# Keys of two sequence tiles multiplied at once, turned as they are made, from blocks of the key matrix that stay in TensorE

## The chip, the cores and the metric

One core of a Trainium2 chip runs the whole program. The metric is device time in microseconds (us) of one execution, the median of several. TensorE (PE) multiplies and turns (transposes) matrices, ScalarE (ACT) and VectorE (DVE) do elementwise work and move results out of TensorE's accumulators, GpSimd (POOL) does small arithmetic, and SyncE (SP) issues the DMAs. Each engine runs its own instructions in order and waits for the others at semaphores.

## The reference, cut to what matters

`x` and `ctx` have 32 tiles of 128 rows and 1024 columns. Each tile passes through four layers:

```
x = x + attention0(layernorm(x), ctx)     # 64-wide queries and keys from ctx, softmax over 1024
x = x + ffn(layernorm(x), routed scales, sign(weight))
x = x + attention1(layernorm(x), ctx)     # Q = text Wq^T + bq, K = ctx Wk^T + bk, 1024 wide
x = x + lora(layernorm(x), routed)
```

The change concerns attention1. Its scores are `(text Wq^T + bq)(ctx Wk^T + bk)^T / 32`. The kernel folds the two weight matrices into one, M = Wk^T Wq, so that per tile it needs "keys through queries", `kw = ctx M` (128 by 1024), and from these the scores `text (kw + bias)^T`.

## The kernel before

The program has a setup, which among other things computes M in two parts, a rounded one (`m_hi`) and a remainder (`m_low`), and then a software pipeline over the 32 tiles. Iteration k prepares tile b = k (queries, keys and values of attention0), attends for tile a = k - 1 (softmax and values of attention0), and runs the chain of the other three layers for tile c = k - 2. Three iterations are unrolled ahead of a hardware loop over the rest, and two after it drain the pipeline. What each engine does in which order is written by hand in its `body`; there is no scheduler.

Products that need precision are split into rounded float32 parts ("hi" and "lo", type F32R), three products for one.

**The keys.** `keys_through_queries` goes through 16 units per tile (two halves of the 1024 columns, eight blocks of 128 rows of M each). A unit is three products of 512 columns: the stationary operand is a turned block of the context (`cT_hi` or `cT_lo`, 128 by 128), the columns that stream are `m_hi`, which lies on chip, or `m_ring`, eight slots into which SP streams the remainder from memory. The units are spread over the first part of an iteration, between the `query_scores` of tile a (`KW_UNITS`). ACT moves the two finished halves to `kw`. In the steps s = 0 to 7 that follow, each with `key_scores`, an exponential on ACT (`prob`), its rounding (`p_hi`), the remainder on DVE (`p_lo`), a running sum (`p_sum`) and `weigh_values` on PE, the kernel turns `kw` on PE, four blocks at s = 4 and four at s = 6, and DVE adds the bias while it moves them to `kwT` (`keys_turned`). At s = 4 the scores of attention1 for tile c read `kwT` of the iteration before.

**The end of an iteration.** At s = 6 ACT takes the softmax of attention1 (`attn`), PE turns it, ACT moves it to `attnT`; between the two ACT normalizes the next tile (`normalize(0)`). At s = 7 PE multiplies `attnT` with the context, makes the queries and keys of tile b (`wqkT`), sums the exponentials with `ones`, turns the context of tile b (`c_in`, eight blocks), and turns the sums (`denominator_columns`) that DVE has moved to `den_wide`. Then come the last `weigh_values`, the turned denominators, the turned `xn_3`, `values` and the first keys' units of tile b. DVE, ahead of `den_wide`, adds the attention to `res` and takes its statistics.

Of the kernel before, what the change touches and what calls it, by code (L numbers as in the profile page):

```python
# [18 lines left out]
F32 = mybir.dt.float32  # L19
# [29 lines left out]
def build(nc, x, ctx_, wq0, bq0, wk0, bk0, wv0, bv0, w_ffn, b_ffn, gate, ics, ocs,  # L49
# [13 lines left out]
    with top:  # L63
# [35 lines left out]
        m_hi = sb("m_hi", [P, T, D], F32R)  # L99
        with ExitStack() as before:  # L100
            wk_nat_late = sb("wk_nat_late", [P, T, HALF], F32, before)
        with ExitStack() as before:
            wk_lo_late = sb("wk_lo_late", [P, T, HALF], F32R, before)
        SLOTS = 8
        m_ring = sb("m_ring", [P, SLOTS, HALF], F32R)
        m_low = nc.dram_tensor("m_low", [2 * T, P, HALF], F32, kind="Internal").ap()
# [16 lines left out]
        with ExitStack() as tmp:  # L123
# [65 lines left out]
            with nc.Block() as block:  # L189
                @block.sync  # L190
                def _(sp):
# [25 lines left out]
                    for n, (kind, i) in enumerate(groups):  # L217
                        if kind == "m":
                            sp.wait_ge(copied, evicted_by_dve(n + 1))
                            sp.dma_start(m_low[(i % 2) * T + f_order[i // 2]],  # L220
                                         m_stage[:, i % STAGES, :].bitcast(F32)).then_inc(m_stored[i % STAGES], 16)
# [9 lines left out]
                    for s in range(STAGES):  # L231
                        sp.wait_ge(m_stored[s], 16 * 2 * T // STAGES)
# [42 lines left out]
                def _(dve):  # L275
# [45 lines left out]
                    for n, (kind, i) in enumerate(groups):  # L321
# [24 lines left out]
                        elif kind == "m":  # L346
                            dve.wait_ge(m_hi_made, i + 1)
                            if i >= STAGES:
                                dve.wait_ge(m_stored[i % STAGES], 16 * (i // STAGES))
# [117 lines left out]
        cT_hi = sb("cT_hi", [P, T, P], F32R)  # L467
        cT_lo = sb("cT_lo", [P, T, P], F32R)

# [6 lines left out]
        kw = x1  # L476
        kwT = sb("kwT", [P, T, P])
# [70 lines left out]
        kwT_done = sem("kwT_done")  # L548
# [33 lines left out]
        kwT_ready = sem("kwT_ready")  # L582
# [37 lines left out]

        def tile4(buf, h):

            return buf[:, 4 * h:4 * h + 4, :].rearrange("p t c -> p (t c)")
# [10 lines left out]
        def iterations(engine, body):  # L634
            for k in range(3):
                body(k, True, k >= 1, k >= 2)
            with engine.Fori(3, NB) as k:
                body(k, True, True, True)
            body(NB, False, True, True)
            body(NB + 1, False, False, True)  # L640

        with nc.Block() as block:
# [3 lines left out]
            def _(sp):  # L646
                def low_unit(u):
                    sp.dma_start(m_ring[:, u % SLOTS, :].bitcast(F32), m_low[u]).then_inc(m_loaded[u % SLOTS], 16)

                def body(k, prepare, attend, chain):  # L650
# [4 lines left out]
                    if attend:  # L655
                        for u in range(12, 16):
                            sp.wait_ge(kw_unit_done, nth(16, a, u - SLOTS + 1))
                            low_unit(u)
                    if prepare:
                        for u in range(SLOTS):  # L660
                            if attend:
                                sp.wait_ge(kw_unit_done, nth(16, a, u + SLOTS + 1))
                            low_unit(u)
                    if prepare and attend:
                        sp.wait_ge(ffn_done, nth(2, c, 2))
                        sp.wait_ge(cT_done, nth(2, b - 1, 2))
                        sp.dma_start(c_in[:, :], ctx_[b]).then_inc(c_loaded, 16)
                        sp.wait_ge(v_done, nth(2, b - 1, 2))
                        sp.dma_start(xn[:, :], x[b]).then_inc(xn_loaded, 16)
                    if attend:  # L670
                        sp.wait_ge(kwT_done, nth(2, a, 2))
                        sp.dma_start(x1[:, :], x[a]).then_inc(x1_loaded, 16)
# [5 lines left out]
                    if prepare:  # L678
                        for u in range(8, 12):
                            sp.wait_ge(kw_unit_done, nth(16, b, u - SLOTS + 1))  # L680
                            low_unit(u)
# [9 lines left out]
            def _(pool):  # L691
# [16 lines left out]
                def body(k, prepare, attend, chain):  # L708
# [20 lines left out]
            def _(act):  # L729
# [27 lines left out]
                def body(k, prepare, attend, chain):  # L757
# [16 lines left out]
                    if attend:  # L774
                        act.wait_ge(kw_unit_done, nth(16, a, 8))
                        act.wait_ge(biased, nth(1, a - 1, 1))
                        nc.scalar.activation(kw[:, half(0)], acc[:, half(0)], ACT.Identity).then_inc(kw_ready, 1)
# [10 lines left out]
                    if attend:  # L788
                        act.wait_ge(kw_unit_done, nth(16, a, 16))
                        nc.scalar.activation(kw[:, half(1)], acc[:, half(1)], ACT.Identity).then_inc(kw_ready, 1)  # L790
                    for s in range(T):
# [41 lines left out]
                    if prepare:  # L833
                        act.wait_ge(cT_done, nth(2, b, 1))
                        act.wait_ge(kw_unit_done, nth(16, b - 1, 16))
                        nc.scalar.activation(tile4(cT_hi, 0), shared[0][:, :], ACT.Identity).then_inc(cT_hi_ready, 1)
                        act.wait_ge(cT_done, nth(2, b, 2))
                        nc.scalar.activation(tile4(cT_hi, 1), shared[1][:, :], ACT.Identity).then_inc(cT_hi_ready, 1)
# [40 lines left out]
            def _(dve):  # L879
# [72 lines left out]
                def keys_turned(a, h):  # L952

                    dve.wait_ge(sc1_done, nth(1, a - 1, 1))
                    dve.wait_ge(kwT_done, nth(2, a, 2 - h))
                    nc.vector.tensor_tensor(kwT[:, 4 * h:4 * h + 4, :], shared[h][:, :].rearrange("p (t c) -> p t c", t=4),
# [516 lines left out]
```

## Time and profile before

| | us |
|---|---|
| median of 3 runs (2147.27 to 2150.97) | 2148.87 |
| the profiled execution's own time | 2148.65 |
| its span, first to last instruction | 2146.7 |
| TensorE busy (matmuls), of the span | 2120.8 |
| VectorE busy | 1852.8 |
| ScalarE busy | 1161.2 |

A matmul's record is longer than the distance to the next one: matmuls are pipelined and their ends are modelled. What a matmul costs in a stream is the distance from start to start. For a group of n records that is (length of the group - length of one) / (n - 1). Weight loads have an engine of their own in the profile (PEld), since they run beside the matmuls.

### The profile page before, as it was taken

To read this page: it belongs to the slowest core of one execution; us is meant where nothing else is said; L and a number is where in the kernel's file an instruction comes from. 1 tells how busy PE (TensorE), PEld (TensorE's weight loads), DVE (VectorE), ACT (ScalarE), POOL (GpSimd) and SP (SyncE) were. 2 spreads that over 40 slices of the span, in tenths; PEclk is the share of its full clock that TensorE was granted. 3 is DMA by queue.
4 is the path that set the end of the run, shared out by engine and by line. 5 is a ranking of instruction groups with operands and counts; after the bars stand their busy time and mean duration, and the time that the engine had idled before them with its cause. 6 is when DMAs were issued, how large, how long until landed. Compare 5 with 4: busy or idle time off the path is not lost.

```text
span 2146.7 us, 35672 instructions
## 1 busy us (share of the span) xinstructions
PE 2120.8 (99%) x11479; PEld 1665.8 (78%) x11479; DVE 1852.8 (86%) x3097; ACT 1161.2 (54%) x1722; POOL 263.8 (12%) x306
## 2 busy tenths in 40 slices
PE   9989999999999999999999999999999999999998
PEld 7867777777777777787777778777777777777776
DVE  8268898988888998888898988889898888899884
ACT  4145555655555565555555655555566555555542
POOL 0011111111101110111111111111111110111010
PEclk9999999999999999999999999999999999999999
DMA  6344343233443323334332333434323344332320
GB/s 215 146 157 128 118 135 103 93 119 127 127 135 119 112 93 107 127 127 137 117 127 100 95 127 117 137 121 133 107 88 117 127 127 137 117 119 93 100 69 30
DMA packets 110874, 254.03 MB, mean 118 GB/s; under 512 B 12976, under 2 KB 14272, under 8 KB 110848
## 3 DMA queue, kind: packets, MB, share of 16 engines
q1 hardware_dynamic: 110848, 253.69, 36.5%
q8 instruction: 16, 0.26, 0.1%
q14 instruction: 10, 0.08, 0.0%
HBM read 215.89 MB, written 20.97 MB: 110 GB/s over the span
## 4 chain that ended last, share of the span: by engine, by line
PE 91%; DVE 1%; ACT 1%; issue 1%; DMA 0%; POOL 0%; DVEq 0%; POOLq 0%; ACTq 0%
PE acc L1239 17%; PE shared L1168 7%; PE scores L1188 6%; PE acc L1199 6%; PE shared L1213 6%; PE acc L1202 6%; PE acc L1200 6%; PE shared L1214 6%; PE scores L1228 5%; PE scores L1227 5%; PE shared L1428 3%; PE shared L1354 3%; PE scores L1174 3%; PE scores L1377 3%; PE scores L1384 1%; PE scores L1404 1%
## 5 line engine op out<-in xcount | busy, mean ns | idle before, releaser
L1033 DVE TENSOR_TENSOR p_lo<-prob,p_hi 128x1024 fp32r<-128x1024 f32 x256 | 312.5, 1221 | 103.7 <-ACT p_hi L805 85.9
L798 ACT ACTIVATE prob<-scores 128x1024 f32<-128x1024 f32 x256 | 260.6, 1018 | 236.6 <-PE scores L1228 185.4
L901 DVE TENSOR_REDUCE neg_max<-scores 128x1 f32<-128x1024 f32 x256 | 307.0, 1221 | 42.1 <-PE scores L1188 35.6
L704 POOL TENSOR_TENSOR rstd<-var_eps,minus_half 128x1 f32<-128x1 f32 x128 | 126.9, 992 | 1732.0 <-DVE var_eps L891 1732.0
L805 ACT ACTIVATE p_hi<-prob 128x1024 fp32r<-128x1024 f32 x256 | 271.2, 1059 | 42.8 <-PE acc L1239 38.6
L1199 PE MATMUL acc<-m_hi,cT_hi 128*128 128x512 f32 x512 | 217.5, 425 | 0.9 <-DVE x L935 0.9
L1213 PE MATMUL shared<-signT,y_hi 128*128 128x512 f32 x512 | 204.5, 399 | 2.2 <-ACT oscale L787 2.2
L1227 PE MATMUL scores<-q_hl,k_hh 128*128 128x512 f32 x512 | 201.4, 393 | 1.9 <-DVE q_m L1015 1.5
L1202 PE MATMUL acc<-m_ring,cT_hi 128*128 128x512 f32 x512 | 202.9, 396 | 0.0
L1200 PE MATMUL acc<-m_hi,cT_lo 128*128 128x512 f32 x512 | 202.4, 395 | 0.0
L1228 PE MATMUL scores<-q_m,k_l 128*128 128x512 f32 x512 | 202.2, 395 | 0.0
L1214 PE MATMUL shared<-signT,y_lo 128*128 128x512 f32 x512 | 201.7, 394 | 0.0
L1041 DVE TENSOR_TENSOR p_sum<-p_sum,prob 128x1024 f32<-128x1024 f32 x160 | 195.1, 1220 | 0.0
L1239 PE MATMUL acc<-p_hi,v_hi 128*128 128x512 f32 x512 | 171.0, 415 | 4.4 <-DVE p_lo L1033 3.9
L1188 PE MATMUL scores<-k_hh,q_hl 128*128 128x512 f32 x512 | 165.4, 404 | 0.3 <-issue 0.3
L1239 PE MATMUL acc<-p_hi,v_lo 128*128 128x512 f32 x512 | 161.0, 396 | 0.0
L1239 PE MATMUL acc<-p_lo,v_hi 128*128 128x512 f32 x512 | 160.9, 395 | 0.0
L1227 PEld LDWEIGHTS scores<-q_hl,k_hh 128*128 128x128 f32 x512 | 96.1, 188 | 25.6 <-issue 1.6
L1188 PEld LDWEIGHTS scores<-k_hh,q_hl 128*128 128x128 f32 x512 | 91.5, 188 | 30.9 <-issue 6.8
L1213 PEld LDWEIGHTS shared<-signT,y_hi 128*128 128x128 f32 x512 | 96.3, 188 | 23.6 <-issue 2.4
L1239 PEld LDWEIGHTS acc<-p_lo,v_hi 128*128 128x128 f32 x512 | 96.0, 188 | 23.5
L1202 PEld LDWEIGHTS acc<-m_ring,cT_hi 128*128 128x128 f32 x512 | 96.2, 188 | 23.2
(241 smaller groups left out, 4211.6 us busy)
## 6 DMA issues: line engine op xcount, KB each, us to landing
m_ring<-m_low SPq DMA_DIRECT2D x512, 256.0 KB, 3.1
c_in<-in_ctx SPq DMA_DIRECT2D x32, 512.0 KB, 3.3
xn<-in_x SPq DMA_DIRECT2D x32, 512.0 KB, 4.1
x<-in_x SPq DMA_DIRECT2D x32, 512.0 KB, 3.2
c_val<-in_ctx SPq DMA_DIRECT2D x32, 512.0 KB, 3.6
out_x<-oscale SPq DMA_DIRECT2D x32, 512.0 KB, 3.0
q_m<-q_hl SPq DMA_DIRECT2D x32, 256.0 KB, 3.1
k_hh<-k_hh SPq DMA_DIRECT2D x32, 256.0 KB, 3.5
```

The costliest lines, as they stand in the source:

```text
L805: nc.scalar.activation(p_hi[s % 2][:, :], prob[s % 2][:, :], ACT.Identity).then_inc(p_hi_ready, 1)
L901: nc.vector.tensor_reduce(neg_max[:, t:t + 1], scores[t % 2][:, :], AX_X, ALU.max, negate=True).then_inc(row_max, 1)
L1033: nc.vector.tensor_tensor(p_lo[s % 2][:, :], prob[s % 2][:, :], p_hi[s % 2][:, :].bitcast(F32), ALU.subtract).then_inc(p_lo_ready, 1)
L1188: last = mm(scores[t % 2][:, half(h)], q_hl[:, t * P:(t + 1) * P], k_hh[:, half(h)], start=True, stop=True)
L1199: mm(acc[:, half(h)], cT_hi[:, f, :], m_hi[:, f, half(h)], start=f == 0, stop=False)
L1200: mm(acc[:, half(h)], cT_lo[:, f, :], m_hi[:, f, half(h)], start=False, stop=False)
L1202: mm(acc[:, half(h)], cT_hi[:, f, :], m_ring[:, u % SLOTS, :], start=False, stop=f == T - 1).then_inc(kw_unit_done, 1)
L1213: mm(shared[h][:, :], y_hi[:, f, :], signT[:, f, half(h)], start=f == 0, stop=False)
L1214: last = mm(shared[h][:, :], y_lo[:, f, :], signT[:, f, half(h)], start=False, stop=f == T - 1)
L1227: mm(scores[s % 2][:, half(h)], k_hh[:, s * P:(s + 1) * P], q_hl[:, half(h)], start=True, stop=False)
L1228: last = mm(scores[s % 2][:, half(h)], k_l1[:, s * P:(s + 1) * P], q_m[:, half(h)], start=False, stop=True)
L1239: last = mm(acc[:, half(h)], v[:, s, :], p[s % 2][:, half(h)], start=first, stop=end)
```

## The change

Tiles are taken in pairs (an even and an odd one), and the keys of both are made together and already turned. The stationary operand of a product is now a 128 by 128 block of M, rounded part or remainder, and what streams is the turned context of the two tiles side by side, 256 columns. Each iteration makes four of the eight feature blocks, for both tiles. A unit has two blocks of rows of M, in both parts, six products; there are 16 units per iteration, as before, and 256 KB per unit, as before. M's rounded part is no longer kept on chip; both parts come through `m_ring`. ACT adds the bias when it moves the finished keys: in an iteration that attends an even tile to `kw_first`, from where an SP DMA copies them to `kwT`, and in the next to `kwT` directly. The turning of `kw` on PE and `keys_turned` on DVE are gone.

Both contexts of a pair must be turned and split before the first of its keys. An iteration with an even tile b therefore turns two contexts: the odd tile's (`c_odd`) at s = 4 and s = 6, and `c_in` at s = 7 as before. An iteration with an odd tile turns none. The hardware loop has two iterations in its body.

```diff
-        SLOTS = 8
-        m_ring = sb("m_ring", [P, SLOTS, HALF], F32R)
+        SLOTS = 8
+        m_ring = sb("m_ring", [P, SLOTS, 2, 2, P], F32R)
+        cT_hi = sb("cT_hi", [P, T, 2, P], F32R)
+        cT_lo = sb("cT_lo", [P, T, 2, P], F32R)
+        kwT = sb("kwT", [P, T, 2, P])
+        kw_first = sb("kw_first", [P, TS, 2, P])
+        c_odd = sb("c_odd", [P, D])
```

SP's queue in an iteration, where `odd` is the parity of tile b:

```diff
+                    if prepare and not odd:
+                        sp.wait_ge(qk_done, nth(2, b - 1, 2))
+                        sp.dma_start(c_odd[:, :], ctx_[b + 1]).then_inc(c_odd_loaded, 16)
...
+                    if attend and odd:
+                        sp.wait_ge(kw_ready, nth(2, a, 2))
+                        sp.wait_ge(sc1_done, nth(1, c, 1))
+                        sp.dma_start(kwT[:, 0:TS, :, :].rearrange("p f j s -> p (f j s)"),
+                                     kw_first[:, :, :, :].rearrange("p f j s -> p (f j s)")).then_inc(kw_moved, 16)
```

ACT's two new functions, and its step s:

```diff
+                def turned_keys(a, odd, h):
+                    act.wait_ge(kw_unit_done, nth(16, a, 8 * h + 8))
...
+                    for f in range(2 * h, 2 * h + 2):
+                        to = kwT[:, TS + f, :, :] if odd else kw_first[:, f, :, :]
+                        last = nc.scalar.activation(to.rearrange("p j s -> p (j s)"), acc[:, f * 2 * P:(f + 1) * 2 * P], ACT.Identity,
+                                                    bias=key_bias[:, TS * odd + f:TS * odd + f + 1])
+                    last.then_inc(kw_ready, 1)
+                def context_rounded(k, j, h, n):
+                    act.wait_ge(cT_done, turned_contexts(k, n))
+                    act.wait_ge(kw_unit_done, nth(16, k - 1, 16))
+                    nc.scalar.activation(of_pair(cT_hi, j, h), bank4(shared[h]), ACT.Identity).then_inc(cT_hi_ready, 1)
...
+                        if chain and prepare and not odd and s == 6:
+                            context_rounded(k, 1, 1, 1)
                         if attend:
                             act.wait_ge(exp_ready, nth(8, a, s + 1))
...
-                        if prepare and attend and s == 6:
+                        if prepare and attend and s == 6 and (odd or not chain):
                             normalize(0, b, xn, xn)
                         if chain and s == 6:
                             act.wait_ge(attnT_done, nth(1, c, 1))
...
+                        if chain and prepare and not odd and s == 6:
+                            context_rounded(k, 1, 0, 2)
+                            normalize(0, b, xn, xn)
```

DVE's step s:

```diff
-                        if attend and s in (4, 6):
-                            keys_turned(a, (6 - s) // 2)
+                        if chain and prepare and not odd and s in (5, 6):
+                            context_remainder(k, 1, 6 - s, s - 4)
```

PE, a unit of the keys, and steps 4, 6 and 7 (`ahead` is `chain and prepare and not odd`):

```diff
-                        mm(acc[:, half(h)], cT_hi[:, f, :], m_hi[:, f, half(h)], start=f == 0, stop=False)
-                        mm(acc[:, half(h)], cT_lo[:, f, :], m_hi[:, f, half(h)], start=False, stop=False)
                         pe.wait_ge(m_loaded[u % SLOTS], nth(32, a, 16 * (u // SLOTS + 1)))
-                        mm(acc[:, half(h)], cT_hi[:, f, :], m_ring[:, u % SLOTS, :], start=False,
-                           stop=f == T - 1).then_inc(kw_unit_done, 1)
+                        to = acc[:, f * 2 * P:(f + 1) * 2 * P]
+                        for j in range(2):
+                            g = 2 * (u % TS) + j
+                            hi, lo = m_ring[:, u % SLOTS, 0, j, :], m_ring[:, u % SLOTS, 1, j, :]
+                            rows_hi, rows_lo = (rows[:, g, :, :].rearrange("p j s -> p (j s)") for rows in (cT_hi, cT_lo))
+                            mm(to, hi, rows_hi, start=g == 0, stop=False)
+                            mm(to, hi, rows_lo, start=False, stop=False)
+                            last = mm(to, lo, rows_hi, start=False, stop=g == T - 1)
+                        last.then_inc(kw_unit_done, 1)
...
-                        if attend and s == 4:
-                            transposes(1, kw, kwT_done)
+                        if ahead and s == 4:
+                            pe.wait_ge(c_odd_loaded, nth(8, b, 16))
+                            transposes(1, c_odd, cT_done)
...
-                        if attend and s == 6:
-                            transposes(0, kw, kwT_done)
+                        if ahead and s == 6:
+                            transposes(0, c_odd, cT_done)
...
-                        if prepare and s == 7:
+                        if prepare and not odd and s == 7:
                             pe.wait_ge(x3_ready, nth(2, c, 2))
```

How it moves instructions, first on PE at s = 4 of the loop's iteration: `kwT` and `key_col` make the scores of attention1, `x` is the buffer in which `kw` lies, and `p_hi`, `p_lo` belong to `weigh_values`. Before:

```order
L1354 MATMUL shared<-kwT,xnT 128x128 x8
L1355 MATMUL shared<-ident,key_col 128x128
L1168 MATMUL shared<-ident,x 128x128 x4
L1239 MATMUL acc<-p_hi,v_hi 128x512 x2
L1239 MATMUL acc<-p_hi,v_lo 128x512 x2
L1239 MATMUL acc<-p_lo,v_hi 128x512 x2
```

and now, in an iteration with an odd tile b:

```order
L1419 MATMUL shared<-kwT,xnT 128x128 x8
L1420 MATMUL shared<-ident,key_col 128x128
L1302 MATMUL acc<-p_hi,v_hi 128x512 x2
L1302 MATMUL acc<-p_hi,v_lo 128x512 x2
L1302 MATMUL acc<-p_lo,v_hi 128x512 x2
```

The four turns between the scores and `weigh_values` are gone there; in an iteration with an even b four turns of `c_odd` stand in their place. It is the same at s = 6. Next, PE at s = 7, from the sums of exponentials (`ones`) to the last `weigh_values`; `xnT` is the buffer of `den_wide`. Before:

```order
L1380 ISA
L1384 MATMUL scores<-p_sum,ones 32x256 x4
L1384 MATMUL scores<-prob,ones 32x256 x4
L1168 MATMUL shared<-ident,c_in 128x128 x8
L1245 MATMUL scores<-ident,xnT 128x128 x2
L1239 MATMUL acc<-p_hi,v_hi 128x512 x2
```

and now, with an odd b:

```order
L1452 ISA
L1456 MATMUL scores<-p_sum,ones 32x256 x4
L1456 MATMUL scores<-prob,ones 32x256 x4
L1308 MATMUL scores<-ident,xnT 128x128 x2
L1302 MATMUL acc<-p_hi,v_hi 128x512 x2
```

The eight turns of `c_in` between the sums and the turned sums are gone; with an even b they stand as before. Third, ACT from the rounding of step 6 to the exponential of step 7 (`prob`). Before:

```order
L805 ACTIVATE p_hi<-prob 128x1024
L813 ACTIVATE r_bias<-r_max 128x1
L816 ACTIVATE attn,r_sum<-shared,r_bias 128x128
L731 REGISTER_ALU
L732 ACTIVATE xn<-xn,shift,rstd 128x1024
L823 ACTIVATE attnT<-shared 128x128
L795 REGISTER_ALU
L797 REGISTER_ALU
L798 ACTIVATE prob<-scores 128x1024
```

and now, in an iteration with an even b:

```order
L811 ACTIVATE cT_hi<-shared 128x4x128
L860 ACTIVATE p_hi<-prob 128x1024
L868 ACTIVATE r_bias<-r_max 128x1
L871 ACTIVATE attn,r_sum<-shared,r_bias 128x128
L878 ACTIVATE attnT<-shared 128x128
L809 REGISTER_ALU
L811 ACTIVATE cT_hi<-shared 128x4x128
L767 REGISTER_ALU
L768 ACTIVATE xn<-xn,shift,rstd 128x1024
L848 REGISTER_ALU
L850 REGISTER_ALU
L851 ACTIVATE prob<-scores 128x1024
```

Two roundings of the odd context (`cT_hi`) came in, and the normalizing of `xn` went from ahead of `attnT` to behind it. With an odd b ACT has the order of before.

## Rows read from the trace of the kernel before

**Rows 1.** The page: span, and each engine's busy time.

```profile
span 2146.7 us, 35672 instructions
...
PE 2120.8 (99%) x11479; PEld 1665.8 (78%) x11479; DVE 1852.8 (86%) x3097; ACT 1161.2 (54%) x1722; POOL 263.8 (12%) x306
```

**Rows 2.** Timeline, steady state, the keys' products: start us, length us, engine, line, operation.

```profile
1001.22 0.40 PE L1199 MATMUL acc<-m_hi,cT_hi 128*128 128x512 f32 x1
1001.22 0.19 PEld L1200 LDWEIGHTS acc<-m_hi,cT_lo 128*128 128x128 f32 x1
1001.46 0.39 PE L1200 MATMUL acc<-m_hi,cT_lo 128*128 128x512 f32 x1
...
1001.91 0.39 PE L1199 MATMUL acc<-m_hi,cT_hi 128*128 128x512 f32 x1
```

**Rows 3.** Groups by line and shape, TensorE: count, busy us in total, mean ns of one.

```profile
L1354 PE MATMUL shared<-kwT,xnT 128*128 128x128 f32 x512 | 62.4, 275 | 0.0
L1377 PE MATMUL scores<-c_in,wqkT 128*128 128x512 f32 x128 | 60.2, 593 | 1.5 <-PEq L189 1.5
...
L1295 PE MATMUL shared<-route3T,ics 96*128 96x128 f32 x256 | 32.3, 269 | 0.0
```

**Rows 4.** The same view for TensorE's weight loads, one line.

```profile
L1354 PEld LDWEIGHTS shared<-kwT,xnT 128*128 128x128 f32 x512 | 62.0, 192 | 2.7
```

**Rows 5.** Page, DMA issues: KB each, us to landing.

```profile
m_ring<-m_low SPq DMA_DIRECT2D x512, 256.0 KB, 3.1
```

**Rows 6.** Timeline of one period, score steps 4 to 7, TensorE, ScalarE and VectorE.

```profile
1025.37 0.60 PE L1168 MATMUL shared<-ident,x 128*128 128x128 f32 x4
...
1025.73 0.71 PE L1239 MATMUL acc<-p_hi,v_hi 128*128 128x512 f32 x2
...
1025.93 1.03 ACT L798 ACTIVATE prob<-scores 128x1024 f32<-128x1024 f32 x1 [1.52 <-DVE p_sum L1041]
...
1027.46 1.06 ACT L805 ACTIVATE p_hi<-prob 128x1024 fp32r<-128x1024 f32 x1 [0.50 <-PE acc L1239]
...
1028.64 0.37 ACT L816 ACTIVATE attn<-shared,r_bias 128x128 f32<-128x128 f32 x1
...
1029.00 1.23 ACT L732 ACTIVATE xn<-xn,shift,rstd 128x1024 f32<-128x1024 f32 x1
...
1029.53 0.27 PE L1364 MATMUL shared<-ident,attn 128*128 128x128 f32 x1
...
1029.64 0.60 PE L1168 MATMUL shared<-ident,x 128*128 128x128 f32 x4
...
1030.14 0.26 ACT L823 ACTIVATE attnT<-shared 128x128 f32<-128x128 f32 x1
...
1030.29 1.03 ACT L798 ACTIVATE prob<-scores 128x1024 f32<-128x1024 f32 x1
...
1032.50 1.23 DVE L1033 TENSOR_TENSOR p_lo<-prob,p_hi 128x1024 fp32r<-128x1024 f32 x1 [0.59 <-DVE r_inv L1070]
```

**Rows 7.** Timeline, the end of that period.

```profile
1033.64 1.40 DVE L1075 SCALAR_TENSOR_TENSOR res<-shared,r_inv,res 128x512 f32<-128x512 f32 x2
...
1036.24 1.09 PE L1168 MATMUL shared<-ident,c_in 128*128 128x128 f32 x8
...
1036.79 0.42 DVE L922 COPY xnT<-scores 128x256 f32<-128x256 f32 x1
...
1037.26 0.44 PE L1245 MATMUL scores<-ident,xnT 128*128 128x128 f32 x2
1037.32 0.60 ACT L836 ACTIVATE cT_hi<-shared 128x512 fp32r<-128x512 f32 x1
...
1039.81 1.22 PE L1168 MATMUL shared<-ident,p_sum 128*128 128x128 f32 x8
```

**Rows 8.** Timeline of the first iteration.

```profile
122.48 3.09 PE L1174 MATMUL scores<-wvT,xn 128*128 128x128 f32 x16 [2.44 <-ACT xn L732]
...
123.08 1.29 DVE L1099 TENSOR_TENSOR cT_lo<-shared,cT_hi 128x512 fp32r<-128x512 f32 x2 [1.85 <-ACT cT_hi L836]
```

More of the change, by code:

```diff
@@ L634, in iterations @@
         def iterations(engine, body):
[L635 to L640, printed above, removed]
+            for k in range(4):
+                body(k, k % 2, True, k >= 1, k >= 2)
+            with engine.Fori(4, NB - 1, 2) as k:
+                body(k, 0, True, True, True)
+                body(k + 1, 1, True, True, True)
+            body(NB, 0, False, True, True)
+            body(NB + 1, 1, False, False, True)
         with nc.Block() as block:
@@ L774, in body @@
                     if attend:
-                        act.wait_ge(kw_unit_done, nth(16, a, 8))
-                        act.wait_ge(biased, nth(1, a - 1, 1))
-                        nc.scalar.activation(kw[:, half(0)], acc[:, half(0)], ACT.Identity).then_inc(kw_ready, 1)
+                        turned_keys(a, 1 - odd, 0)
                     if chain:
@@ L788, in body @@
                     if attend:
-                        act.wait_ge(kw_unit_done, nth(16, a, 16))
-                        nc.scalar.activation(kw[:, half(1)], acc[:, half(1)], ACT.Identity).then_inc(kw_ready, 1)
+                        turned_keys(a, 1 - odd, 1)
                     for s in range(T):
@@ L832, in body @@
                         normalize(0, b, xn, xn)
[L833 to L838, printed above, removed]
+                    if prepare and not attend:
+                        context_rounded(k, 1, 1, 1)
+                        context_rounded(k, 1, 0, 2)
+                    if prepare and not odd:
+                        context_rounded(k, 0, 0, 3)
+                        context_rounded(k, 0, 1, 4)
                     if attend and not prepare:
@@ L1095, in body @@
                         denominators_inverse(a)
-                    if prepare:
-                        for h in range(2):
-                            dve.wait_ge(cT_hi_ready, nth(2, b, h + 1))
-                            nc.vector.tensor_tensor(tile4(cT_lo, h), shared[h][:, :], tile4(cT_hi, h).bitcast(F32),
-                                                    ALU.subtract).then_inc(cT_lo_ready, 1)
+                    if prepare and not attend:
+                        context_remainder(k, 1, 1, 1)
+                        context_remainder(k, 1, 0, 2)
+                    if prepare and not odd:
+                        context_remainder(k, 0, 0, 3)
+                        context_remainder(k, 0, 1, 4)
                     if attend:
@@ L1257, in out_products, with body @@
                     mm(banks[1], lowT_lo[:, :], bT_hi[:, half(1)], start=False, stop=True).then_inc(out_done, 1)
-                def body(k, prepare, attend, chain):
+                def body(k, odd, prepare, attend, chain):
                     b, a, c = k, k - 1, k - 2
+                    ahead = chain and prepare and not odd
                     last_chain = chain and not attend
```

130 lines of the change are left out of this document (79 added, 51 removed).

## The prediction

> **What bounds the kernel now.** I read the page first. TensorE is busy for 2120.8 of 2146.7 us, VectorE for 1852.8, ScalarE for 1161.2 [rows 1]. The reader is to see that nothing can be gained that does not shorten TensorE's own chain, and that VectorE has so little to spare that places may exist where TensorE just manages not to wait for it. So I read two things next: what one matmul costs in a stream, and, in the timeline of one steady iteration, who releases whom where the change adds or removes work. The profiled execution took 2148.65 us, 0.2 below the median of 2148.87; all sums below start from 2148.65. A difference under 0.2% (4.3 us) is what a measurement here can hardly tell from none.
>
> **The keys' products.** Before, a unit is three products of 512 columns, and the next unit starts 0.69 us after this one's start (1001.22 to 1001.91), so a product costs 0.23 us [rows 2]. An iteration has 16 units, 11.04 us. Now it has 96 products of 256 columns: the same columns, twice as many weight loads. The question is what a product of half the length costs, and the trace has no such row. The neighbours, with the distances worked out from the groups: the scores with `kwT` are unsplit float32, 16 records in each of 32 groups, 62.4 / 32 = 1.95 us, so (1.95 - 0.275) / 15 = 0.112 us per pass of 128 columns, each pass with a load of 128 by 128. The context with `wqkT` (4 records in 1.88 us) gives 0.429 us per pass of 512. The routed scales (`ics`, F32R by the code, 8 in 1.01 us) give 0.106 us for 128 columns [rows 3]. So a load can be had every 0.112 us and less, although one load's record is 192 ns long: 512 of them fill only 62.0 us [rows 4], they overlap each other and the matmuls. The passes of unsplit float32 grow by (0.429 - 0.112) / 384 = 0.000826 us per column; an F32R product streams in about half of that, 0.211 us for 512 columns, which leaves 0.019 us of the 0.23 that could be a fixed price per product.
>
> The ends: 0.106 us, if a half-length product goes as fast as the loads do (96 x 0.106 = 10.18 us, 0.86 less per iteration, 28 us less over 32); 0.125 us, if the 0.019 us is fixed (12.0 us, 0.96 more, 31 us more over 32). I take 0.115, half of the long product: the unsplit passes change weights as often, and the line through their two lengths leaves only 0.112 - 128 x 0.000826 = 0.006 us fixed, so the rest seems to go with the F32R columns. By this the term is **0**.
>
> The load of the next product's weights starts at the same time as the product itself (both 1001.22), and the next product follows 0.24 us later, less than load and product one after the other [rows 2]. The Trainium skill ("TensorE: Matmul & The Clock Gate", Part 3, The mechanism) says that a weight load overlaps a running matmul only when the two are in different row groups; here all use the whole array, so each load would stand alone, and 48 more of them per iteration would be paid in full. This trace does not agree with that. The Trainium skill gives in the same page (LDWEIGHTS) columns / 1.2 ns for a load, 107 ns for 128 columns; an estimate from it is that load and product of 256 columns would be about equally long, and the sum by it that of the lower end.
>
> **The ring.** Both parts of M now come through it, in units as large and as many as before; one lands 3.1 us after its issue [rows 5], and eight slots are 5.5 us of keys at least. Only the first two products of a unit lose their freedom to start ahead of the landing. 0 taken. The copy from `kw_first` and the load of `c_odd` are needed half an iteration or more after their issue: 0.
>
> **Iterations with an odd b.** No turns stand at s = 4, 6 and 7. The four at s = 4 held `weigh_values` up from 1025.37 to 1025.73, 0.36 us. ACT's rounding of step 6 waits for that `weigh_values` (1027.46, idle 0.50 for PE's `acc`), so it comes 0.36 earlier, and after it all that ACT does in one chain: `attn` 1028.64, `normalize` 1029.00, `attnT` 1030.14, the exponential of step 7 at 1030.29; then DVE's `p_lo` at 1032.50, which had idled 0.59 [rows 6]. From there DVE goes on without a gap: `res` 1033.64, statistics, `den_wide` 1036.79 to 1037.21, and PE's turned sums start at 1037.26 [rows 7]. So the turned sums wait for DVE's chain, not for the eight turns of `c_in` ahead of them (1036.24, 1.09 us), which only fill that wait. Removing those, and the four at s = 6, moves PE's wait and not its end: of about 1.8 us of turns, 0.36 us counts. Behind it, the turns of `xn_3` no longer wait for the remainder of a context (1.22 us for eight where `c_in` has 1.09): 0.13 more. Sum **-0.49 us** for each of 15 such iterations, -7.4 us. VectorE's `keys_turned` and two remainders are gone too, but the chain above hangs on ACT there, so this is hidden.
>
> **Iterations with an even b.** PE has the same turns at the same places. ACT gets two roundings of 0.60 us (the length of `cT_hi` in [rows 7]) and another order, and the chain above runs over ACT. The first rounding follows the exponential of step 6 (1025.93, done 1026.96) and fills most of ACT's idle 0.50: the rounding `p_hi` goes from 1027.46 to 1027.6. `attn` is done at 1029.15. Now `attnT` is next, and PE turns `attn` at 1029.53 to 1029.80, because `weigh_values` stands ahead of it: ACT idles until 1029.9, a gap that `normalize` used to fill. Then the second rounding has to wait for the turns of `c_odd` (1029.64 to 1030.24), runs 1030.34 to 1030.94, and `normalize` comes only then, at 1030.91. Before, what followed `normalize` on ACT (`attnT` then) started 1.14 us after it (1029.00 to 1030.14); now the exponential of step 7 follows. So it starts at 1032.05 in place of 1030.29: 1.76 us late [rows 6]. Late next are `p_lo` of step 7 (DVE waits on it in order), `res`, the statistics, `den_wide` (1038.55), the turned sums (1039.02), and with them the last `weigh_values`, the turned denominators, `xn_3` and `values`, which PE runs without a wait from there [rows 7]. `c_in` waits for `res` until 1036.9 and is done by 1038, inside that wait. Sum **+1.76 us** for each of 15 such iterations (k = 2 to 30), +26.4 us.
>
> **The ends of the pipeline.** In the first iteration both contexts are turned, rounded and split one after the other, through the same two accumulators: `values` stood at 122.48, the remainders of the one context at 123.08 to 124.37 [rows 8]; the second context's turns (1.04 us, by the distance of `c_in` to the next in [rows 7]: 1.02) come behind these, so `values` starts at about 125.5: **+3.0 us**. Iterations 1 and 32 lose key turns: -0.5 each as above, -1.0. The setup stores M's rounded part too, in shorter rows; its products take all the time there: 0, at most some 3 us (a landing of [rows 5]).
>
> **Sum.** 26.4 - 7.4 + 3.0 - 1.0 + 0 = +21.0 us: 2148.65 + 21.0 = 2169.7, **2170 us**.
>
> **Rivals.**
> *The half-length product goes at 0.106 us.* For it: the `ics` row, which is F32R and has that distance. Against it: those products have 96 rows and 128 columns, so they show loads and not a stream of 256. Then 2170 - 28 = 2142 us, faster; the time falls 0.2% below the old one from 0.107 us down.
> *Loads don't hide behind half-length products.* Product and load one after the other would be 0.115 + 0.112 = 0.227 us, 96 of them 21.8 us, 10.75 us more per iteration, 344 us: 2514 us. Against it: 0.112 us for load and pass together [rows 3]. (By the rule of the Trainium skill on row groups, "TensorE: Matmul & The Clock Gate", Part 3, it would come out this way.)
> *The even iterations' slip is swallowed*, because PE has other work to wait for or ACT gets ahead: then only the odd ones change, 2148.65 - 7.4 + 2.0 = 2143 us. Against it: DVE's `den_wide` ends 0.05 us ahead of the turned sums; there is no slack that could swallow it.
>
> **How the numbers follow.** Forecast 0.66, with 2155 to 2201 us by the ends of the half-length product that still end slower; rival one 0.08, loads not hidden 0.07, slip swallowed 0.07; 0.08 for a mixture that ends within 0.2% of before, 0.04 for slower ones between. So faster 0.15, same 0.08, slower 0.77. The range is 2142 to 2205: it reaches down to the first two faster cases and up to the higher price of the product with the setup's 3 us; below it lie some 0.09, above it, with the unhidden loads, 0.10.
>
> **What the profile after would show.** The distance between products of 256 columns at the keys' line: 0.115 us or another. Iterations alternating, the even longer by about 2.2 us than the odd. In the even ones, ACT's `normalize` after the second `cT_hi`, PE idle about 1 us ahead of the turned sums, and the exponential of step 7 some 1.8 us later behind the turning of `attn`. In the odd ones PE idle ahead of the turned sums too, for `den_wide`. The prediction is wrong if the half-length product costs other than 0.106 to 0.125 us, or if PE's wait at the turned sums does not follow ACT's step 7.

## The result, and the profile after

The changed kernel takes 2166.73 us (median of 4 runs, 2165.79 to 2166.94), the kernel before in the same session 2148.07 (4 runs, 2146.58 to 2150.97): ratio 1.0084, 95% interval 1.0067 to 1.0102. It is slower by 0.8%, where 2170 us was forecast.

The page of the changed kernel: span, busy time of each engine, and the shares of the chain that ended last.

```profile
span 2163.9 us, 37822 instructions
...
PE 2093.0 (97%) x12759; PEld 1728.1 (80%) x12759; DVE 1812.5 (84%) x3033; ACT 1179.5 (55%) x1786; POOL 264.3 (12%) x306
...
PE 75%; DVE 11%; issue 6%; ACT 3%; ACTq 0%; DVEq 0%; POOL 0%; POOLq 0%
```

Against [rows 1], TensorE has 28 us less work and the span is 17.2 us longer: TensorE now waits. To see where, I use one instruction as a mark, the turn of the row maxima, which each iteration has once. Its rows in the timeline of before, and then of after (start, length, engine, line):

```profile
940.72 0.27 PE L1314 MATMUL scores<-ident,neg_max 128*8 128x128 f32 x1
...
1002.79 0.27 PE L1314 MATMUL scores<-ident,neg_max 128*8 128x128 f32 x1
...
1064.85 0.27 PE L1314 MATMUL scores<-ident,neg_max 128*8 128x128 f32 x1
```

```profile
950.22 0.27 PE L1378 MATMUL scores<-ident,neg_max 128*8 128x128 f32 x1
...
1013.92 0.27 PE L1378 MATMUL scores<-ident,neg_max 128*8 128x128 f32 x1
...
1075.44 0.27 PE L1378 MATMUL scores<-ident,neg_max 128*8 128x128 f32 x1
```

Before, every iteration takes 62.07 us. After, one with an even tile b takes 63.70 (950.22 to 1013.92) and one with an odd tile 61.52, and so through the whole steady part (means 63.71 and 61.53): +1.64 and -0.54. All of the steady loss lies in the even ones.

Steps 6 and 7 of that even iteration, timeline of after; the times to compare are distances from the mark (here 950.22, in [rows 6, 7] 1002.79):

```profile
974.90 1.06 ACT L860 ACTIVATE p_hi<-prob 128x1024 fp32r<-128x1024 f32 x1
...
976.08 0.37 ACT L871 ACTIVATE attn<-shared,r_bias 128x128 f32<-128x128 f32 x1
...
977.26 0.28 ACT L878 ACTIVATE attnT<-shared 128x128 f32<-128x128 f32 x1 [0.71 <-PE shared L1431]
...
977.69 0.60 ACT L811 ACTIVATE cT_hi<-shared 128x512 fp32r<-128x512 f32 x1 [0.16 <-PE shared L1224]
...
978.19 1.23 ACT L768 ACTIVATE xn<-xn,shift,rstd 128x1024 f32<-128x1024 f32 x1
...
979.32 1.01 ACT L851 ACTIVATE prob<-scores 128x1024 f32<-128x1024 f32 x1
...
981.51 1.23 DVE L1088 TENSOR_TENSOR p_lo<-prob,p_hi 128x1024 fp32r<-128x1024 f32 x1 [2.18 <-issue]
...
985.79 0.42 DVE L980 COPY xnT<-scores 128x256 f32<-128x256 f32 x1
...
986.27 0.44 PE L1308 MATMUL scores<-ident,xnT 128*128 128x128 f32 x2 [1.06 <-DVE xnT L980]
...
988.82 1.22 PE L1224 MATMUL shared<-ident,p_sum 128*128 128x128 f32 x8
```

`p_hi` of step 6 and `attn` stand where they stood (24.68 and 25.86 us after the mark; before 24.67 and 25.85). Then ScalarE idles 0.71 for the turn of `attn`, rounds the context, and only then normalizes. The exponential of step 7 starts 29.10 after the mark, before 27.50: 1.60 late. `p_lo` is 1.58 late, the wide denominators (the copy to `xnT`, L980) 1.57, the turned sums at L1308 1.58, the turns of `xn_3` (they lie in the buffer `p_sum`, L1224) 1.58. The loss is handed on whole from ScalarE over VectorE to TensorE.

The end of the odd iteration that follows, same view (mark 1013.92):

```profile
1047.48 0.42 DVE L980 COPY xnT<-scores 128x256 f32<-128x256 f32 x1
...
1047.96 0.44 PE L1308 MATMUL scores<-ident,xnT 128*128 128x128 f32 x2 [1.11 <-DVE xnT L980]
...
1050.51 1.04 PE L1224 MATMUL shared<-ident,p_sum 128*128 128x128 f32 x8
```

The turned sums start 34.04 after the mark, before 34.47, and TensorE waits 1.11 for them although no turn is left ahead of them. The waits of TensorE in the whole of after (waiting line, releaser, us in total, times, longest) say the same of both kinds:

```profile
PE scores L1308 <- DVE xnT L980: 33.1, 31, 1.1
```

Before had no such wait of TensorE in its list. No landing of `m_ring` or `kwT` stands in the list of after either, so the ring and the copy cost TensorE no wait that the profile shows. The keys' products of after, grouped by line, and a few in the timeline:

```profile
L1263 PE MATMUL acc<-cT_hi,m_ring 128*128 128x256 f32 x1024 | 302.6, 296 | 0.9 <-DVE x L993 0.9
L1264 PE MATMUL acc<-cT_lo,m_ring 128*128 128x256 f32 x1024 | 288.6, 282 | 0.0
...
L1264 PEld LDWEIGHTS acc<-cT_lo,m_ring 128*128 128x128 f32 x1024 | 194.5, 190 | 7.4
```

```profile
1012.71 0.28 PE L1263 MATMUL acc<-cT_hi,m_ring 128*128 128x256 f32 x1
1012.83 0.28 PE L1264 MATMUL acc<-cT_lo,m_ring 128*128 128x256 f32 x1
1012.95 0.28 PE L1265 MATMUL acc<-cT_hi,m_ring 128*128 128x256 f32 x1
```

One product of 256 columns follows the other after 0.12 us, with a load whose record is 0.19 us long. The loads are hidden: 3072 products that each stood behind their load would show in these distances.

### The profile page after: what moved, and what is told of

Same layout as the page of the kernel before. It is cut to its first block, busy times and chain, and to the rows that moved or that the text cites. A ratio compares the mean times of both kernels' runs of the same rounds, so it can differ in the third digit from the quotient of the medians.

```text
span 2163.9 us, 37822 instructions
## 1 busy us (share of the span) xinstructions
PE 2093.0 (97%) x12759; PEld 1728.1 (80%) x12759; DVE 1812.5 (84%) x3033; ACT 1179.5 (55%) x1786; POOL 264.3 (12%) x306
## 4 chain that ended last, share of the span: by engine, by line
PE 75%; DVE 11%; issue 6%; ACT 3%; ACTq 0%; DVEq 0%; POOL 0%; POOLq 0%
PE acc L1302 11%; PE scores L1244 6%; PE acc L1263 6%; PE shared L1276 6%; PE acc L1264 6%; PE acc L1265 6%; PE shared L1277 5%; PE shared L1224 5%; PE scores L1291 5%; PE scores L1290 5%; DVE p_lo L1088 3%; PE shared L1506 3%; PE scores L1230 3%; DVE res L1130 2%; DVE stat L945 1%
## 5 line engine op out<-in xcount | busy, mean ns | idle before, releaser
L1263 PE MATMUL acc<-cT_hi,m_ring 128*128 128x256 f32 x1024 | 302.6, 296 | 0.9 <-DVE x L993 0.9
L1264 PE MATMUL acc<-cT_lo,m_ring 128*128 128x256 f32 x1024 | 288.6, 282 | 0.0
L1265 PE MATMUL acc<-cT_hi,m_ring 128*128 128x256 f32 x1024 | 288.5, 282 | 0.0
L1263 PEld LDWEIGHTS acc<-cT_hi,m_ring 128*128 128x128 f32 x1024 | 195.7, 191 | 8.5 <-DVE x L993 1.1
L1264 PEld LDWEIGHTS acc<-cT_lo,m_ring 128*128 128x128 f32 x1024 | 194.5, 190 | 7.4
L1265 PEld LDWEIGHTS acc<-cT_hi,m_ring 128*128 128x128 f32 x1024 | 194.2, 190 | 0.0
```

The lines of the kernel that those rows point to most:

```text
L1263: mm(to, hi, rows_hi, start=g == 0, stop=False)
L1264: mm(to, hi, rows_lo, start=False, stop=False)
L1265: last = mm(to, lo, rows_hi, start=False, stop=g == T - 1)
```

## The experiments

The theory was the prediction's: ScalarE's order at step 6 of the even iterations (normalize behind `attnT` and a rounding) makes the exponential of step 7 late, and that is what the even iterations lose; the odd ones gain the four turns of step 4, the other turns being idle time of TensorE anyway. The rivals: ScalarE's order is covered by other waits, and the loss is the turning of a second context on TensorE or VectorE, or the half-length products.

All times below are medians; the ratio is to the kernel before in the same session.

**Normalize ahead again.** Edit to the changed kernel:

```diff
-                        if prepare and attend and s == 6 and (odd or not chain):
+                        if prepare and attend and s == 6:
                             normalize(0, b, xn, xn)
...
                             context_rounded(k, 1, 0, 2)
-                            normalize(0, b, xn, xn)
```

> In iterations with an even b ACT normalizes the next tile ahead of attnT again, as in the kernel before; the second rounding of the odd context stays behind attnT. Theory (the even iterations are longer because ACT idles between attn and attnT and then does the second rounding and normalize ahead of the exponential of step 7): that exponential comes at about 1031.0 instead of some 1.6 us after its old place of 1030.29, so 0.7 us late instead of 1.6; 0.9 us off each of 15 even iterations, 13.5 us: about 2153 us. Rival (the time went to the half-length products or to the ring, and ACT's order is beside the way): no change, 2165 to 2168 us.

Measured 2150.53 us, ratio 1.0012 (1.0002 to 1.0022): 16.2 us less than the changed kernel. Timeline of this kernel, even iteration, mark at 945.09:

```profile
971.31 1.23 ACT L768 ACTIVATE xn<-xn,shift,rstd 128x1024 f32<-128x1024 f32 x1
...
972.44 0.27 ACT L878 ACTIVATE attnT<-shared 128x128 f32<-128x128 f32 x1
...
972.60 0.60 ACT L811 ACTIVATE cT_hi<-shared 128x512 fp32r<-128x512 f32 x1
...
973.08 1.03 ACT L851 ACTIVATE prob<-scores 128x1024 f32<-128x1024 f32 x1
...
980.04 0.44 PE L1307 MATMUL scores<-ident,xnT 128*128 128x128 f32 x2 [0.41 <-DVE xnT L979]
```

Normalize runs in the gap in which TensorE turns `attn`, and ScalarE does not idle. The exponential starts 27.99 after the mark, 0.49 later than before, and the turned sums 0.48 later. What is left fits the one rounding that still stands ahead of it (972.60 to 973.08, 0.48 from start to start). The even iteration takes 62.60, 1.11 less than in the changed kernel; the odd one 61.52, unchanged.

**Normalize last.** Normalize goes behind the rounding of step 7's probabilities, in every iteration, and the second rounding behind the exponential of step 7:

```diff
-                        if chain and prepare and not odd and s == 6:
-                            context_rounded(k, 1, 1, 1)
+                        if chain and prepare and not odd and s >= 6:
+                            context_rounded(k, 1, 7 - s, s - 5)
...
+                        if prepare and attend and s == 7:
+                            normalize(0, b, xn, xn)
...
-                        if prepare and attend and s == 6 and (odd or not chain):
-                            normalize(0, b, xn, xn)
...
-                        if chain and prepare and not odd and s == 6:
-                            context_rounded(k, 1, 0, 2)
-                            normalize(0, b, xn, xn)
```

> ACT normalizes the next tile behind the rounding of step 7 in all iterations, where it waits for the queries otherwise, and the second rounding of the odd context stands between the exponential and the rounding of step 7. Nothing is left out. Theory: attnT follows attn as soon as PE has turned it, the exponential of step 7 comes about 0.3 us ahead of its old place, and the second rounding costs 0.6 behind it. Even iterations then end some 0.35 us behind those of the kernel before instead of 1.64, odd ones 0.3 us earlier than now, -0.86 instead of -0.55: 1.6 us for each of 15 pairs, 24 us: about 2143 us. Rival (ACT's order is beside the way): 2165 to 2168 us. A middle result, 2150 to 2158, if VectorE and not ACT holds step 7 once ACT is early.

Measured 2140.39 us, ratio 0.9968 (0.9956 to 0.9979). It is the only version of the changed kernel with all its work that pays: 26.3 us below the changed kernel and 7.5 below the kernel before in its session (2147.87). Timeline of this kernel, even iteration, mark at 940.13:

```profile
967.18 0.28 ACT L878 ACTIVATE attnT<-shared 128x128 f32<-128x128 f32 x1 [0.73 <-PE shared L1428]
...
967.39 1.03 ACT L851 ACTIVATE prob<-scores 128x1024 f32<-128x1024 f32 x1
...
968.32 0.59 ACT L811 ACTIVATE cT_hi<-shared 128x512 fp32r<-128x512 f32 x1
...
968.79 1.06 ACT L860 ACTIVATE p_hi<-prob 128x1024 fp32r<-128x1024 f32 x1
...
969.74 1.24 ACT L768 ACTIVATE xn<-xn,shift,rstd 128x1024 f32<-128x1024 f32 x1
969.90 1.02 PE L1437 MATMUL shared<-c_val,attnT 128*128 128x512 f32 x2
969.94 1.23 DVE L1085 TENSOR_TENSOR p_lo<-prob,p_hi 128x1024 fp32r<-128x1024 f32 x1 [0.24 <-DVE r_inv L1122]
```

`p_lo` starts 29.81 after the mark; before it was 29.71. The even iteration is back at 62.21, the odd one at 61.29.

**No odd context in the even iterations.** The turns, roundings and remainders of `c_odd` are left out from the second pair on, so the odd tiles' keys are made from tile 1's context; `normalize` stands as before. Of the edit, the TensorE part (the ScalarE and VectorE calls for it go too):

```diff
-                        if ahead and s == 4:
-                            pe.wait_ge(c_odd_loaded, nth(8, b, 16))
-                            transposes(1, c_odd, cT_done)
...
-                        if ahead and s == 6:
-                            transposes(0, c_odd, cT_done)
```

> Leaves out, from the second pair on, the turning, rounding and splitting of the odd tile's context (PE, ACT and DVE), with ACT's order as in odd iterations; the odd tiles' keys are then made from the context of tile 1. The half-length products, the ring and all DMAs stay. Theory: the even iterations lose their 1.6 us and gain 0.4 as the odd ones do at step 4, 2.0 us for each of 15, 30 us: about 2136 us, less than the kernel before. Rival (half-length products or ring): the eight turns on PE alone, at most 0.9 us for each of 15 iterations, 13 us: about 2153 us, not less than before.

Measured 2136.57 us, ratio 0.9949 (0.9933 to 0.9966). The even iterations take 61.68, the odd ones 61.52: with the second context gone, both kinds are alike within 0.16 us. So little else costs the even iterations anything, and of the 30.2 us between this and the changed kernel, 16.2 are ScalarE's order alone (the run with normalize ahead) and 14 the turning, rounding and splitting.

**Idle turns in the odd iterations.** Two kernels, each the changed one with turns of `c_odd` that nobody reads: eight at step 7, and four at step 4.

```diff
+                        if prepare and odd and chain and s == 7:
+                            pe.wait_ge(x3_ready, nth(2, c, 2))
+                            for h in range(2):
+                                transposes(h, c_odd, idle_turns)
```

> Adds to each iteration with an odd b eight turns of c_odd, read by nobody, at the place where the turns of c_in stood before. Theory (PE waits there for den_wide, so that the turns which went were worth nothing): no change, 2165 to 2168 us. Rival (each turn removed was worth its time on PE): 1.02 us for each of 15 iterations more, about 2182 us.

Measured 2166.61 us, ratio 1.0089 (1.0072 to 1.0105): no change, and the iterations take 63.71 and 61.53 as in the changed kernel. TensorE's waits in this kernel:

```profile
PE scores L1309 <- DVE xnT L981: 16.5, 16, 1.1
```

The wait is gone from 15 of its 31 places and the time stays: eight turns there fill the wait and nothing else.

```diff
+                        if chain and prepare and odd and s == 4:
+                            transposes(1, c_odd, idle_turns)
```

> The changed kernel, with four turns added that nobody reads, of the odd context, at step 4 of the odd iterations. Theory (the 0.5 us that an odd iteration gains is that of the four turns that are gone from step 4, not of those from steps 6 and 7): 0.3 to 0.45 us more in each of 15 odd iterations, 2171 to 2174. Rival (TensorE waits later for the wide denominators anyway, as it does in the odd iterations with the turns added at step 7): no change, 2166 to 2168.

Measured 2172.76 us, ratio 1.0110 (1.0095 to 1.0125): 6.0 us more than the changed kernel's 2166.73. The odd iterations go from 61.53 to 61.96, the even ones stay at 63.71. Four turns at step 4 cost 0.43 us each time, eight at step 7 nothing. The odd iteration of the changed kernel (mark at 1013.92) and then of this one (mark at 1016.52) in the timeline:

```profile
1038.16 1.06 ACT L860 ACTIVATE p_hi<-prob 128x1024 fp32r<-128x1024 f32 x1
...
1043.20 1.22 DVE L1088 TENSOR_TENSOR p_lo<-prob,p_hi 128x1024 fp32r<-128x1024 f32 x1 [1.36 <-issue]
```

```profile
1041.18 1.06 ACT L861 ACTIVATE p_hi<-prob 128x1024 fp32r<-128x1024 f32 x1 [0.50 <-PE acc L1303]
...
1046.22 1.22 DVE L1089 TENSOR_TENSOR p_lo<-prob,p_hi 128x1024 fp32r<-128x1024 f32 x1 [1.51 <-issue]
...
1050.98 0.44 PE L1309 MATMUL scores<-ident,xnT 128*128 128x128 f32 x2 [1.26 <-DVE xnT L981]
```

The rounding of step 6 waits for `weigh_values` again (0.50, as in [rows 6]) and starts 24.66 after the mark, in the changed kernel 24.24. `p_lo` of step 7 is 0.42 later as well (29.70 for 29.28), and the turned sums 0.42 (34.46 for 34.04). TensorE still waits 1.26 there: the four turns did not use the wait up, they moved its end.

**Normalize last in the kernel before**, a control for the version that pays:

```diff
+                        if prepare and attend and s == 7:
+                            normalize(0, b, xn, xn)
...
-                        if prepare and attend and s == 6:
-                            normalize(0, b, xn, xn)
```

> The kernel before, with one thing moved: ScalarE's normalize of the next tile stands behind the rounding of step 7's probabilities, instead of ahead of step 6's, in every iteration. Theory (in the kernel before the turns of the context at step 7 and the wide denominators end within 0.1 us of each other ahead of the turned sums, so that an earlier exponential of step 7 gains next to nothing while the turns are there): no change to 0.1 us less per iteration, 2145 to 2149. Rival (ScalarE's order alone is worth what it gave behind the change, 0.3 us in each iteration): about 2138.

Measured 2147.13 us against 2149.56 in the same session, ratio 0.9986 (0.9977 to 0.9995); the iterations take 62.00 for 62.07. The order alone is worth 0.07 us there, and behind the change 0.24 in the odd iterations (61.53 to 61.29). So most of what the version that pays gains is not an old gain of ScalarE's order that the kernel before could have had: by the profiled spans (2138.1 and 2145.2) it is 0.3% under the control, by the ratios of the two sessions (0.9968 and 0.9986) 0.2%. The intervals of the two ratios just meet (0.9956 to 0.9979 and 0.9977 to 0.9995), so the times alone leave the size of that open; in the profiles an even and an odd iteration together take 123.50 us there, 124.00 in the control and 124.14 in the kernel before.

**Half-length products in the kernel before.** Each of the 48 key products of 512 columns is cut in two; the loop around them:

```diff
+                        for r in range(2):
+                            to = slice(h * HALF + r * 2 * P, h * HALF + (r + 1) * 2 * P)
+                            mm(acc[:, to], cT_hi[:, f, :], m_hi[:, f, to], start=f + r == 0, stop=False)
+                            mm(acc[:, to], cT_lo[:, f, :], m_hi[:, f, to], start=False, stop=False)
...
+                            last = mm(acc[:, to], cT_hi[:, f, :], m_ring[:, u % SLOTS, r * 2 * P:(r + 1) * 2 * P],
+                                      start=False, stop=f + r == T)
```

> The kernel before, with each of the 48 products of 512 columns that make an iteration's keys cut into two of 256 columns on the same stationary, loaded twice; all else as it was. Theory (a half-length product costs 0.120 us from start to start where the whole one costs 0.231 to 0.237, by the traces of both kernels): 0.15 to 0.30 us more per iteration, so 2153 to 2158. Rival (a half-length product costs 0.115 or less, what the prediction took, and the 0.005 belongs to other things in the changed kernel): 2148 or less.

Measured 2148.93 us against 2149.56, ratio 1.0000 (0.9991 to 1.0009). My expectation missed. The lines of its products:

```profile
L1201 PE MATMUL acc<-m_hi,cT_hi 128*128 128x256 f32 x1024 | 302.8, 296 | 0.9 <-DVE x L935 0.9
L1202 PE MATMUL acc<-m_hi,cT_lo 128*128 128x256 f32 x1024 | 288.0, 281 | 0.0
```

They are as in the changed kernel, and the median distance is 0.119 us there. Summed from each key product's start to the start of what follows it, an iteration's keys take 12.08 us where the kernel before has 11.93 (after: 12.11). The iteration itself grows by 0.02 only (62.07 to 62.09). So the rival's time came, but not by its reason: a half-length product does cost more than half, and most of that sum does not reach the iteration's length. The eleven stretches of keys of an iteration start at the same distance from the mark in both kernels within 0.06 us on average, nine of them within 0.04, so the excess of the stretches (up to 0.04 each) does not add up; what stands between them, and takes it up, names no wait in TensorE's list, and stays open. The equal time hides one thing more: the stretch behind the last mark, where nothing was changed, is 1.6 us shorter in the profiled run of this kernel (87.13 for 88.75), for reasons that stand under the ends below.

## Why the prediction was right

Three things carried it, and each now has a run or a trace behind it.

**The even iterations, +1.76 forecast, +1.64 measured.** The mechanism was right link by link (distances from the mark): `attnT` forecast at 27.1, measured 27.04; the second rounding 27.55, measured 27.47; normalize 28.12, measured 27.97; the exponential of step 7 29.26, measured 29.10. The turned sums were forecast 1.76 late and were 1.58 late. The first rounding did not push `p_hi` of step 6 by 0.14 as I had it, and did not push `attn`; that changed nothing, since ScalarE waits for the turn of `attn` behind it. What made the link shorter is that `attnT` and normalize each followed 0.07 sooner on what they wait for. Putting normalize ahead takes 1.11 us of it back by itself, moving the second rounding and normalize behind the exponential all but 0.14: the order on ScalarE is shown as the cause, and that the second context is turned in these iterations at all is the rest.

**The odd iterations, -0.49 forecast, -0.54 measured.** The four turns of step 4 were taken at 0.36, by their distance in [rows 6]; adding them back costs 0.43, and by the chain that was named. The 0.07 between the two is that I counted from the first turn: from the product with `key_col` ahead of the turns to `weigh_values` it is 0.58 us before (1025.15 to 1025.73) and 0.14 in the changed kernel (1036.28 to 1036.42). The turns of `xn_3` were to gain 0.13 and take 1.04 where the even ones take 1.22. The turns of steps 6 and 7 were taken at nothing; for step 7 the run with eight idle turns shows it. For those of step 6 there is no run of their own.

**The half-length product, taken at 0.115 us, 0.120 measured.** This was the widest term of the range, and both rivals that hung on it fell. At 0.106 the time would have been 2142. Loads that do not hide would have made 2514: this trace contradicts that, with 0.12 us from product to product and a load record of 0.19. The Trainium skill ("TensorE: Matmul & The Clock Gate", Part 3, The mechanism) has the rule by which it would have come out so, that a load overlaps a running matmul only in another row group; this trace does not agree with it. The same section also lets a load go ahead of running matmuls into a background weight buffer, and that these distances do not contradict.

The size was a little low. Half of the long product leaves out a fixed part, and the two lengths show one, 2 x 0.120 - 0.234 = 0.006 us (0.234 is the median distance before), a third of the 0.019 that the upper end of the range was built on. The keys' sum is 0.18 us longer per iteration (12.11 against 11.93); taken as paid in full, that would have been 6 us. In the odd iteration above, `values` start 0.61 sooner (0.43 and the 0.18 of `xn_3`), and the next mark comes 0.54 sooner: 0.07 is lost between them. Averaged over the steady part it is 0.05, and 0.05 in the even iterations too (1.59 late at `values`, 1.64 at the mark). So the term of 0 was right within 0.02 to 0.07 us per iteration, and by luck in part: that a half-length product costs just half is not what the distances show, and why most of the excess does not reach the iteration's length is open. The third rival, a slip that is swallowed, fell with the 1.58 us at the turned sums.

**The ends.** Here the sizes were off, in both directions. From the start to the second mark the profiled runs differ by 2.7 us (the first mark stands at 144.35 for 140.95, the interval to the second is 0.69 shorter); forecast 2.5. The first iteration of after:

```profile
121.26 1.09 PE L1224 MATMUL shared<-ident,c_odd 128*128 128x128 f32 x8 [1.77 <-DMA c_odd<-in_ctx]
...
124.83 1.94 PE L1224 MATMUL shared<-ident,c_in 128*128 128x128 f32 x8 [2.48 <-DVE cT_lo L1012]
...
126.57 2.72 PE L1230 MATMUL scores<-wvT,xn 128*128 128x128 f32 x16
```

The two contexts do go one after the other through the same accumulators, and `values` start at 126.57, against 122.48 [rows 8], 1.1 later than the 125.5 forecast. That the second context's turns wait for the remainders of the first was in the forecast, and they start at 124.83 where I had 124.4. The larger part of the miss is the clock: from the first of the eight turns to `values` it is 1.74 us, where I had 1.04. One stretch of that trace (from and to, its length, TensorE's busy time and matmuls, granted clock, DMA share, GB/s):

```profile
124.80:128.10 3.30, 3.27 (x16) 0.50 0.99 289
```

The granted clock is 0.50 there, 1.2 of 2.4 GHz, after TensorE had waited 1.77 us, run the eight turns of `c_odd` and waited 2.48 us. The kernel before has such a stretch too (123.3 to 126.6, also 0.50), but at its `values` and first keys. Of the 4.1 us at `values`, 3.4 are left at the first mark.

At the other end, from the last mark on, the changed kernel is 2.1 us shorter (86.61 for 88.75) where I had 0.5. All eight turns of `kw` count there at first, 0.82 us at the products with `attnT` (28.18 us behind the last mark for 29.00). But TensorE then waits longer for VectorE's `den_inv` (0.87 for 0.54), and 0.50 is left at the turned denominators (33.74 for 34.24): the forecast. The other 1.6 us come later and are not the turns'. Before, and then after:

```profile
2096.09 3.79 PE L1428 MATMUL shared<-lowT,xnT 128*128 128x136 f32 x16
...
2110.78 1.09 ACT L787 ACTIVATE oscale<-shared 128x512 f32<-128x512 f32 x2 [2.22 <-DMA out_x<-oscale]
```

```profile
2114.94 2.12 PE L1506 MATMUL shared<-lowT,xnT 128*128 128x136 f32 x16
...
2127.97 1.08 ACT L841 ACTIVATE oscale<-shared 128x512 f32<-128x512 f32 x2 [0.96 <-DMA out_x<-oscale]
```

The sixteen products with `lowT` ran at a granted clock of 0.50 before (2096.2 to 2099.5) and at 1.00 after; some 0.4 us of that reaches what follows. ScalarE's `oscale` waited 2.22 us for a store to land before and 0.96 after, which is the other 1.2; why the store lands sooner stays open. The kernel before with half-length products, in which nothing of this stretch was changed, has neither (clock 1.00, a wait of 1.00), and is 1.6 us shorter there as well. So these 1.6 us are not shown to be the change's; without them its end is as forecast.

The account of the profiled runs closes: +2.7 at the start, 15 x 1.64 = +24.6, 15 x -0.54 = -8.1, -2.1 at the end, together +17.1; the spans differ by 17.2. Forecast were +2.5, +26.4, -7.4, -0.5, together +21.0.

## What to carry to other kernels

When work moves from one engine to another, write out the order of the third engine that both wait for: here TensorE was relieved of 28 us of work and the kernel became 19 us longer, mostly because one ScalarE instruction was issued behind a wait whose gap it used to fill. In an in-order queue, put what nobody waits for soon (normalize) behind what the longest chain waits for (the exponential), and look at the step where the chain begins rather than where the bound engine idles. The gain depends on what the chain waits for: the same move was worth 0.07 us per iteration in the kernel before. And price a removed instruction by its place: the same turns cost 0.43 us per four at one step and nothing per eight at another.

## What was not expected of the hardware

Cutting 48 products of 512 columns per iteration into 96 of 256, each with its own 128 by 128 load, left the time unchanged (ratio 1.0000, 0.9991 to 1.0009). The median distance went from 0.234 us per product to 0.119 per half, while a load's record is 0.19 us long: records of loads overlap each other and the products. An iteration grew by 0.02 us.
